# A fused decoder layer (state-space scan, cross attention, quantized FFN) on one core: PSUM slots given job by job in the prologue, side results of the scan taken later

## The chip, the cores and the metric

The kernel runs on one NeuronCore of a Trainium2 chip, as one launch. The metric is the device time of that core in microseconds. The engines are PE (TensorE, matrix multiplies and transposes into PSUM), DVE (VectorE), ACT (ScalarE), POOL (GpSimd) and SP (SyncE, which here issues every DMA). Each engine works through its own instructions in the order in which they are written and waits on semaphores for the others.

## The reference

The input is 8 x 128 x 256 in float32. The state-space block takes the first axis as its time (8 steps) and the 128 rows as its batch; the attention takes the first axis as its batch. A tile t = 0..7 below is one entry of that first axis, 128 rows.

```python
def reference(x, ctx_512, ...):
    x = _layernorm(x + attn_ref(x, ...))        # state-space block
    x = _layernorm(x + xattn_ref(x, ctx, ...))  # cross attention, 16 heads, rope, latent q and k
    x = _layernorm(x + ffn_ref(x, w_up, w_down))# Hadamard, 8-bit activations, ternary weights

def attn_ref(...):
    xz = einsum('ed,lbd->bel', in_proj_w, h);  x, z = split(xz)
    x  = silu(sum_k conv_w[:, k] * shift(x, k))           # 4 taps
    x_dbl = einsum('ed,bdl->bel', x_proj_w, x)            # 128 low-rank rows, 16 B, 16 C
    delta = softplus(dt_proj_w @ x_dbl[:128] + dt_proj_b)
    A = -exp(A_log)                                       # 512 channels x 16 states
    def step(h, t):
        h = exp(delta_t * A) * h + (delta_t * u_t) * B_t  # 16 states
        y = einsum('bdn,bn->bd', h, C_t)
        return h, y
    y = (scan(step) + x * D) * silu(z)
    return out_proj_w @ y

def weight_quant(w):                                      # used for w_up and w_down
    scale = clip(mean(abs(w)), EPS, None)
    return clip(round(w / scale), -1, 1) * scale
```

## The kernel before

The program has three stages, each written out for every engine: the prologue (0 to about 91 us), the scan (to about 280 us), and the attention with the FFN (to the end).

**Prologue.** PE works through a list `jobs` (L236 to L238; the loop that issues them begins at L395). A job writes one pair of PSUM banks, and there are four pairs. X0 to X3 are the input projection of four channel blocks; Z0 to Z3 the gate projection; DTR the low-rank sum over the four convolved blocks (it waits for `silu_s` k+1 before block k); FF the sum that gives the scales of the ternary weights; DT0 to DT3 the step sizes of two tiles each; BC and BCT the B and C rows and their transpose; UD0 to UD3 the skip term u times D; TU0 to TU3 the transposes of u. A job's pair is its place in the list modulo 4 (`pair`, L251), so a job waits until the job four places ahead of it has been taken out of PSUM; `freed` holds which engine takes it and its count. ACT takes Z (`gates`, L733, a Silu into a two-slot buffer that SP stores to DRAM), DTR (L748) and UD (`skips`, L767, also stored by SP). DVE takes the rest: `biased(p)` (L1088) for DT, `step_inputs(p)` (L1112) for TU.

`squares_of(p)` (L753, ACT: Abs, Exp, four Squares) and `softplus(p)` (L1096, DVE: L1103, three times L1105, L1107, L1110) make delta of two tiles, p = 0..3. Square 0 of p waits for L1107 of p-1, since both use one buffer. `ternary(i)` (L1079, DVE, three operations of 1024) rounds w_up (i = 0) and w_down (i = 1). Silu and Exp need different tables of ACT, so there is a table load at each change between `gates` and `squares_of`.

SP stores gates and skips in a written order, then issues `zeros` (2 MB into Nw), `load_m(0)` and `load_m(1)`, waits for all stores to have landed, and only then issues `stage(0)`: the loads of `ud_t` (the stored skip term of the tile), `zs_t` (its gates) and `x_t`.

**Scan.** Seven steps, t = 1..7, of 16 states each. Per state n of step t:

- POOL `arg` (L973): delta times A for two states at a time, into a ring of four;
- ACT `decay(t, n)` (L779): Exp, into one of four PSUM banks; it waits until the state four back has been added;
- DVE `state_decay` (L1160, L1157 in step 1) and `state_add` (L1167): the new state;
- ACT `weigh(t, n)` (L787): state times C into the ring `hc` of four slots; it is issued three states late (`BEHIND`), and waits until PE has used the state four back (`y_s`);
- PE `state_sum` (L497): four transposes that add it onto the tile's sum in PSUM.

PE begins a step with `skip_sum(t)`, which waits for the load of `ud_t` (`st_u`) and for DVE's `gate(t-1)` (L1175, after state 3), since the sum's bank is only free then. After `state_sum` of n = 3 PE does `out_proj(t-1)`, after n = 11 `turn_x1(t-1)`. DVE's norm of the tile before stands after n = 9 and n = 11. I call the start of L1175 the gate of a step; the time from gate to gate is the length of a step.

Four side jobs per step prepare the attention's merged weights: P0 to P3 (step 1), KV0, KV1, N0, N1 (step 2), N2 to N5 (step 3), M0 to M15 (steps 4 to 7). PE issues side job i of a step after the `state_sum` of state `PE_SIDE[i]`, and ACT takes its result (`take_side`, L815; the copies are L825 to L839) after the `decay` and `weigh` of iteration `ACT_SIDE[i]`. Two banks alternate.

SP's order in the scan's iteration t: `stage(t)` (ud_t after `skip_sum(t-1)`, zs_t after `gate(t-1)`, x_t after `out_proj(t-1)`); loads of w_q and w_kcq for later M jobs that wait for side job 0 or 1 of this step; the store of x1; in t = 1 the loads of w_qr and w_kr, which wait for P3; then the loads that wait for side job 2 or 3 (in t = 4, 5 and 6, for M3, M7 and M11).

**Attention and FFN.** PE `project` (L594) waits first for every side result (`pe.wait_ge(side_e, len(side))`). These 32 slots and the FFN are untouched but for one insertion.

```python
PE_SIDE = (0, 4, 8, 10)
ACT_SIDE = (5, 9, 13, 15)
```

## Time and profile before

| | us |
|---|---|
| median of three runs | 568.6 (565.62 to 569.82) |
| the profiled execution's own time | 569.41 |
| its span | 567.2 |
| PE busy (share of the span) | 453.4 (80%) |
| DVE busy | 401.4 (71%) |
| ACT busy | 311.0 (55%) |
| POOL busy | 216.7 (38%) |
| mean granted clock of PE, 1 is 2.4 GHz | 0.874 |

The span runs from the first to the last instruction; 2.2 us lie around it. A wait in brackets behind an instruction is its engine's idle time and what ended it. "PE ps L386" is every matmul that is issued through one helper; its tile names tell the job. A matmul of float32 counts as two records.

### The profile page before, as it was taken

How to read it: one execution, taken by the hardware profiler on the slowest of the kernel's cores; microseconds unless marked ns; L12 is line 12 of the kernel's file. 1: busy time of each engine (PE TensorE's matmuls, PEld its weight loads, DVE VectorE, ACT ScalarE, POOL GpSimd, SP SyncE). 2: the span in 40 equal slices, each digit the busy share in tenths (PEclk: the TensorE clock that was granted, in tenths of full speed). 3: DMA queues.
4: the chain of work that ended last, by engine and by line, in shares of the span. 5: the costliest groups of instructions: out<-in, count | busy, mean ns of one | idle time of the engine just before them, and what ended most of it. 6: DMA issues, size and time to landing. Idle time of an engine off the chain costs nothing.

```text
span 567.2 us, 9787 instructions
## 1 busy us (share of the span) xinstructions
PE 453.4 (80%) x3240; PEld 368.8 (65%) x3248; DVE 401.4 (71%) x722; ACT 311.0 (55%) x717; POOL 216.7 (38%) x157
## 2 busy tenths in 40 slices
PE   4999622858787757566799999999999999998733
PEld 2446422547575645546688889898888888897522
DVE  0949499788678879797754567777777677777443
ACT  2548782769587869696524353444545353444310
POOL 2300037495839486876042323123223223223010
PEclk9999855877575969897999999999999999999765
DMA  8960491040101123031200000000000000000000
GB/s 288 360 223 37 138 337 40 13 121 25 34 9 46 54 68 103 20 102 29 70 20 2 10 1 2 19 0 18 0 18 0 0 18 0 18 0 20 0 9 9
DMA packets 18649, 32.38 MB, mean 57 GB/s; under 512 B 2112, under 2 KB 11712, under 8 KB 17792
## 3 DMA queue, kind: packets, MB, share of 16 engines
q1 hardware_dynamic: 18624, 32.06, 17.0%
q8 instruction: 14, 0.23, 0.2%
q14 instruction: 11, 0.09, 0.1%
HBM read 25.73 MB, written 6.32 MB: 57 GB/s over the span
## 4 chain that ended last, share of the span: by engine, by line
PE 40%; DVE 24%; issue 19%; ACT 10%; POOL 4%; DMA 1%; DVEq 1%; POOLq 0%; ACTq 0%; SPq 0%
PE ps L386 32%; PE ps L497 5%; DVE reg_b L1167 4%; ACT hc L787 4%; DVE reg_b L1105 3%; DVE ps L1160 2%; POOL reg_b L999 2%; PE ps L594 2%; ACT ps L779 2%; ACT reg_b L869 2%; POOL small L978 1%; DVE reg_b L1220 1%; DVE ps L1157 1%; DMA Nw<-x_fm 1%; DVE reg_b L1219 1%
## 5 line engine op out<-in xcount | busy, mean ns | idle before, releaser
L973 POOL TENSOR_TENSOR reg_b<-reg_c,reg_a 128x1024 f32<-128x1024 f32 x56 | 131.1, 2370 | 82.4 <-DVE reg_c L1110 61.1
L999 POOL TENSOR_TENSOR reg_b<-reg_b 128x768 f32<-128x768 f32 x32 | 58.0, 1813 | 140.1 <-DVE reg_b L1220 107.4
L497 PE MATMUL ps<-ident,hc 128*128 128x128 f32 x452 | 86.2, 331 | 29.0 <-ACT hc L787 28.8
L497 PEld LDWEIGHTS ps<-ident,hc 128*128 128x128 f32 x452 | 62.7, 169 | 48.5 <-ACT hc L787 45.1
L386 PE MATMUL ps<-x1T,Mw 128*128 (+1 forms) x768 | 93.5, 278 | 0.0
L386 PEld LDWEIGHTS ps<-x1T,Mw 128*128 128x128 f32 x768 | 88.2, 192 | 3.4 <-issue 0.6
L787 ACT ACTIVATE hc<-reg_b,bc 128x512 f32<-128x512 f32 x112 | 79.8, 713 | 12.8 <-DVE reg_b L1167 12.3
L1160 DVE TENSOR_TENSOR ps<-ps,reg_b 128x512 f32<-128x512 f32 x96 | 66.0, 691 | 26.1 <-ACT ps L779 26.1
L1167 DVE SCALAR_TENSOR_TENSOR reg_b<-reg_c,bc,ps 128x512 f32<-128x512 f32 x112 | 81.9, 736 | 0.0
L869 ACT ACTIVATE reg_b<-ps,small 128x128 f32<-128x128 f32 x128 | 45.3, 366 | 40.0 <-DVE small L1225 39.3
L779 ACT ACTIVATE ps<-reg_b 128x512 f32<-128x512 f32 x112 | 65.7, 588 | 0.7 <-POOL reg_b L973 0.7
L386 PE MATMUL ps<-reg_b,Nw 128*64 128x128 f32 (+1 forms) x512 | 55.7, 283 | 0.3 <-POOL reg_b L999 0.3
L978 POOL TENSOR_TENSOR small<-small 128x1 f32<-128x1 f32 x24 | 13.2, 550 | 110.8 <-DVE small L1185 110.8
L876 ACT ACTIVATE reg_b<-ps 128x512 f32<-128x512 f32 x32 | 19.1, 597 | 63.3 <-PE ps L594 63.3
L386 PEld LDWEIGHTS ps<-reg_b,Nw 128*64 128x64 f32 (+1 forms) x512 | 45.3, 165 | 7.0 <-issue 3.8
L386 PE MATMUL ps<-reg_b 128*64 128x128 f32 (+1 forms) x512 | 43.5, 294 | 2.7 <-ACT reg_b L863 0.5
L497 PE MATMUL ps<-ident,ud_t 128*128 128x128 f32 x32 | 8.9, 434 | 40.8 <-DVE yT L1175 24.9
L386 PEld LDWEIGHTS ps<-reg_b 128*64 128x64 f32 (+1 forms) x512 | 32.3, 166 | 12.5 <-ACT reg_b L863 8.0
L1225 DVE TENSOR_REDUCE small<-ps 128x4 f32<-128x512 f32 x32 | 22.0, 688 | 22.6 <-PE ps L386 22.5
L386 PE MATMUL ps<-Nw 128*128 128x512 f32 x64 | 30.0, 627 | 7.2 <-DMA Nw<-x_fm 7.1
L497 PEld LDWEIGHTS ps<-ident,ud_t 128*128 128x128 f32 x32 | 5.7, 217 | 43.9 <-DVE yT L1175 22.4
L1219 DVE TENSOR_TENSOR reg_b<-ps,reg_a 128x768 f32<-128x768 f32 x32 | 30.4, 951 | 2.9 <-PE ps L386 2.9
(137 smaller groups left out, 714.2 us busy)
## 6 DMA issues: line engine op xcount, KB each, us to landing
reg_a<-a_dram SPq DMA_DIRECT2D x4, 1024.0 KB, 7.9
Mw<-w_o SPq DMA_DIRECT2D x1, 2048.0 KB, 16.2
zs_dram<-x1T SPq DMA_DIRECT2D x4, 512.0 KB, 3.7
ud_dram<-reg_b SPq DMA_DIRECT2D x4, 512.0 KB, 3.0
Nw<-zeros SPq DMA_DIRECT2D x1, 2048.0 KB, 9.6
mring<-w_q SPq DMA_DIRECT2D x8, 256.0 KB, 3.1
ud_t<-ud_dram SPq DMA_DIRECT2D x8, 256.0 KB, 3.5
zs_t<-zs_dram SPq DMA_DIRECT2D x8, 256.0 KB, 3.4
```

What stands on the lines that cost most here:

```text
L386: return pe.matmul(o, l, r, start=start, stop=stop)
L497: return pe.matmul(o, src, ident[:, :], start=start, stop=stop, is_transpose=True, skip_group_check=True)
L779: act.activation(ps[:, n % RING, :], dA[:, n // SA % RING, n % SA, :], ACT.Exp, scale=-1.0).then_inc(da_s, 1)
L787: act.activation(hc[:, (n + 1) % WRING, :], H[:, n, :], ACT.Copy, scale=bc[:, t, s:s + 1]).then_inc(hc_s, 1)
L869: last = act.activation(prob[:, g % 2, h, :], scores_of[:, h % 2, h // 2, :], ACT.Exp, bias=negm[:, g % 2, h:h + 1], accum_out=sums[:, g % ...
L876: act.activation(probT[:, g % 2].rearrange("p h n -> p (h n)"), ps[:, 4, :], ACT.Copy).then_inc(pte, 1)
L973: pool.tensor_tensor(dA[:, g % RING], delta_r[:, bass.ds(t, 1), :].to_broadcast([P, SA, DI]), Abc[:, g * SA:(g + 1) * SA, :], ALU.mult).th ...
L999: pool.tensor_tensor(rq[:, g % 2].rearrange("p a c n -> p (a c n)"), pc[:, g % 2].rearrange("p a c n -> p (a c n)"), psn[:, g % 2].rearran ...
L1160: dve.tensor_tensor(E_n, E_n, H[:, n, :], ALU.mult).then_inc(dah_s, 1)
L1167: dve.scalar_tensor_tensor(H[:, n, :], step_du(t), step_b(t, n), ps[:, n % RING, :], ALU.mult, ALU.add).then_inc(h_s, 1)
L1219: dve.tensor_tensor(pc[:, g % 2], v, ropeq_s[:, 0], ALU.mult)
L1225: dve.tensor_reduce(negm[:, g % 2].rearrange("p (i e) -> p e i", e=2), scores_of, AX.X, ALU.max, negate=True).then_inc(mx, 1)
```

## The change

- `jobs` has a new order, with DTR directly behind X3, Z0 and Z1 behind UD1, Z2 and Z3 behind TU1, and each job's pair of banks is now given in a table, `slot_of`. A job waits for the last holder of its pair.
- ACT's order in the prologue: the gates 0 and 1, then skips 2 and 3, then both remaining `squares_of`, then gates 2 and 3. SP stores in the same order.
- DVE: `ternary(0)` stands ahead of `biased(0)`; `ternary(1)` has left the prologue. Its weights are loaded again after the scan (SP, 512 KB), and it runs between the first and the second eight-slot group of the attention.
- POOL waits for all four deltas before its first `arg`, no longer for the first alone.
- Scan: PE issues side jobs after states 4, 8, 12, 15; ACT takes them in iterations 11 and 15 of the step and 2 and 6 of the next (the last two of all after the scan).

```diff
-PE_SIDE = (0, 4, 8, 10)
-ACT_SIDE = (5, 9, 13, 15)
+PE_SIDE = (4, 8, 12, 15)
+ACT_SIDE = (11, 15, NST + 2, NST + 6)
...
-        jobs = row("X", *range(CI)) + row("Z", 0) + row("DTR", 0) + row("FF", 0) + row("DT", 0, 1) + row("BC", 0)
-        jobs += row("DT", 2) + row("BCT", 0) + row("DT", 3) + row("UD", 0, 1, 2) + row("Z", 1, 2, 3) + row("UD", 3)
-        jobs += row("TU", *range(T // 2))
+        jobs = row("X", *range(CI)) + row("DTR", 0) + row("FF", 0) + row("DT", 0, 1, 2) + row("BC", 0)
+        jobs += row("DT", 3) + row("BCT", 0) + row("UD", 0, 1) + row("Z", 0, 1) + row("UD", 2, 3)
+        jobs += row("TU", 0, 1) + row("Z", 2, 3) + row("TU", 2, 3)
+        slot_of = dict(zip(jobs, (0, 1, 2, 3, 0, 1, 3, 1, 0, 2, 3, 1, 3, 1, 2, 0, 3, 1, 3, 1, 2, 0, 3, 1)))
...
-                if j >= 4:
-                    who, n = freed[jobs[j - 4]]
+                if before[job]:
+                    who, n = freed[before[job]]
...
-            store_gates(0)
             store_skip(0)
             store_skip(1)
+            store_gates(0)
+            store_gates(1)
             store_skip(2)
-            for p in range(1, CI):
-                store_gates(p)
             store_skip(3)
+            store_gates(2)
+            store_gates(3)
             sp.wait_ge(pe_job, pos[("Z", CI - 1)] + 1)
             sp.dma_start(nw_flat, zeros).then_inc(ld["zero"], 16)
...
             sp.dma_start(had_s, had).then_inc(ld_had, 16)
+            sp.dma_start(wdn_again, w_dn).then_inc(ld_wdn, 16)
...
-            gates(0)
             gated(3)
...
             squares_of(0)
             skips(0)
+            skips(1)
             squares_of(1)
-            skips(1)
+            gates(0)
+            gates(1)
             skips(2)
+            skips(3)
             squares_of(2)
-            gates(1)
+            squares_of(3)
             gates(2)
             gates(3)
-            skips(3)
-            squares_of(3)
...
                     if n in ACT_SIDE:
                         take_side(per_step * (t - 1) + ACT_SIDE.index(n))
+                    if carried and NST + n in ACT_SIDE:
+                        take_side(per_step * (t - 2) + ACT_SIDE.index(NST + n))
...
+            for j in range(len(side) - sum(n >= NST for n in ACT_SIDE), len(side)):
+                take_side(j)
             take_x1(T - 1)
...
-            pool.wait_ge(delta_s, 1)
+            pool.wait_ge(delta_s, T // 2)
...
+            ternary(0, wup_raw, wupq[:, :, :])
             biased(0)
             biased(1)
+            biased(2)
             take(("BC", 0))
...
-            ternary(0, wup_raw, wupq[:, :, :])
-            biased(2)
+            biased(3)
             take(("BCT", 0))
...
-            ternary(1, wdn_raw, wdnq[:, :, :])
+            softplus(1)
...
             slots(0, True, False, False, lag=False, scan_end=True)
+            dve.wait_ge(ld_wdn, 16)
+            ternary(1, wdn_again, wdnq[:, :, :])
             slots(1, True, True, False)
```

PE in the prologue, before. `Nw 128x512` is X or Z (four rows a job), `reg_b,Pw 128x512` DTR, `small,x` FF, `zs_t,Pw` DT (two a job), `32x256` BC, `x_t` BCT, `ud_t,reg_b` UD (eight a job), `ident,reg_b` TU (eight a job):

```order
L386 MATMUL ps<-Nw 128x512 x20
L386 MATMUL ps<-reg_b,Pw 128x512 x8
L386 MATMUL ps<-small,x 128x2
L386 MATMUL ps<-zs_t,Pw 128x512 x4
L386 MATMUL ps<-reg_b,Pw 32x256 x16
L386 MATMUL ps<-zs_t,Pw 128x512 x2
L428 MATMUL ps<-ident,x_t 128x128 x2
L386 MATMUL ps<-zs_t,Pw 128x512 x2
L386 MATMUL ps<-ud_t,reg_b 128x128 x24
L386 MATMUL ps<-Nw 128x512 x12
L386 MATMUL ps<-ud_t,reg_b 128x128 x8
L456 MATMUL ps<-ident,reg_b 128x128 x32
```

The same engine and place in the changed kernel:

```order
L396 MATMUL ps<-Nw 128x512 x16
L396 MATMUL ps<-reg_b,Pw 128x512 x8
L396 MATMUL ps<-small,x 128x2
L396 MATMUL ps<-zs_t,Pw 128x512 x6
L396 MATMUL ps<-reg_b,Pw 32x256 x16
L396 MATMUL ps<-zs_t,Pw 128x512 x2
L438 MATMUL ps<-ident,x_t 128x128 x2
L396 MATMUL ps<-ud_t,reg_b 128x128 x16
L396 MATMUL ps<-Nw 128x512 x8
L396 MATMUL ps<-ud_t,reg_b 128x128 x16
L466 MATMUL ps<-ident,reg_b 128x128 x16
L396 MATMUL ps<-Nw 128x512 x8
```

Z0 has left the place ahead of DTR, and the first two TU jobs now stand ahead of Z2 and Z3; the last two TU jobs follow these rows.

ACT in the prologue, before, from the Squares of p = 0 on (L764 Squares, L770 skips, L757 and L759 Abs and Exp, L736 gates):

```order
L764 ACTIVATE reg_b<-reg_b,small 128x1024 x4
L770 ACTIVATE reg_b<-ps 128x1024 x2
L757 ACTIVATE reg_b<-reg_c 128x1024
L759 ACTIVATE reg_b<-reg_b 128x1024
L764 ACTIVATE reg_b<-reg_b,small 128x1024 x4
L736 ACT_TABLE_LOAD
L736 ACTIVATE x1T<-ps 128x1024 x3
L770 ACTIVATE reg_b<-ps 128x1024
L757 ACTIVATE reg_b<-reg_c 128x1024
L759 ACT_TABLE_LOAD
L759 ACTIVATE reg_b<-reg_b 128x1024
L764 ACTIVATE reg_b<-reg_b,small 128x1024 x4
```

ACT in the changed kernel, from the Squares of p = 1 on (L773 Squares, L779 skips, L766 and L768 Abs and Exp, L746 gates):

```order
L773 ACTIVATE reg_b<-reg_b,small 128x1024 x4
L746 ACT_TABLE_LOAD
L746 ACTIVATE x1T<-ps 128x1024 x2
L779 ACTIVATE reg_b<-ps 128x1024 x2
L766 ACTIVATE reg_b<-reg_c 128x1024
L768 ACT_TABLE_LOAD
L768 ACTIVATE reg_b<-reg_b 128x1024
L773 ACTIVATE reg_b<-reg_b,small 128x1024 x4
L766 ACTIVATE reg_b<-reg_c 128x1024
L768 ACTIVATE reg_b<-reg_b 128x1024
L773 ACTIVATE reg_b<-reg_b,small 128x1024 x4
L746 ACT_TABLE_LOAD
```

Both pairs of gates now come with a table load of their own; gates 2 and 3 are behind every Square.

PE in step 1 of the scan, before (`ident,ud_t` skip_sum, `ident,hc` state_sum, four a state, `Mw 64x256` a P job, `w_out_s,yT` out_proj):

```order
L497 MATMUL ps<-ident,ud_t 128x128 x4
L497 MATMUL ps<-ident,hc 128x128 x4
L386 MATMUL ps<-Mw 64x256 x4
L497 MATMUL ps<-ident,hc 128x128 x12
L386 MATMUL ps<-w_out_s,yT 128x256 x4
L497 MATMUL ps<-ident,x_t 128x128 x2
L497 MATMUL ps<-ident,hc 128x128 x4
L386 MATMUL ps<-Mw 64x256 x4
L497 MATMUL ps<-ident,hc 128x128 x16
L386 MATMUL ps<-Mw 64x256 x4
```

The same step in the changed kernel, from out_proj to its end:

```order
L396 MATMUL ps<-w_out_s,yT 128x256 x4
L507 MATMUL ps<-ident,x_t 128x128 x2
L507 MATMUL ps<-ident,hc 128x128 x4
L396 MATMUL ps<-Mw 64x256 x4
L507 MATMUL ps<-ident,hc 128x128 x16
L396 MATMUL ps<-Mw 64x256 x4
L507 MATMUL ps<-ident,hc 128x128 x12
L540 MATMUL ps<-ident,x 128x128 x2
L507 MATMUL ps<-ident,hc 128x128 x4
L396 MATMUL ps<-Mw 64x256 x4
L507 MATMUL ps<-ident,hc 128x128 x12
L396 MATMUL ps<-Mw 64x256 x4
```

No job stands ahead of out_proj any more, and the fourth one is now the last thing in the step, directly ahead of the next skip_sum. SP's own order in the scan is the same in both.

## Rows read from the trace of the kernel before

**Rows 1.** Gate to gate: length; PE, PEld, DVE, ACT, POOL busy; PE clock; DMA share, GB/s

```profile
96.72:123.90 27.18, 19.18 (x112) 12.99 (x112) 22.67 (x39) 20.76 (x37) 19.07 (x10) 0.81 0.28 68
123.90:151.00 27.10, 21.94 (x104) 18.26 (x104) 22.22 (x39) 21.13 (x39) 20.27 (x10) 0.63 0.09 31
151.00:181.40 30.40, 25.01 (x112) 20.17 (x112) 22.24 (x39) 22.59 (x44) 19.22 (x10) 0.61 0.10 26
...
206.90:232.50 25.60, 16.72 (x96) 13.70 (x96) 22.03 (x39) 20.34 (x37) 19.22 (x10) 0.89 0.23 67
...
258.02:279.58 21.56, 16.78 (x98) 13.98 (x99) 16.49 (x29) 15.47 (x28) 6.90 (x4) 0.87 0.21 65
```

**Rows 2.** The page's costliest groups: busy, mean ns, idle before and its releaser

```profile
L1160 DVE TENSOR_TENSOR ps<-ps,reg_b 128x512 f32<-128x512 f32 x96 | 66.0, 691 | 26.1 <-ACT ps L779 26.1
```

**Rows 3.** Timeline, start of step 7: start, us, engine, line, [idle before <-releaser]

```profile
258.75 1.12 PE L497 MATMUL ps<-ident,ud_t 128*128 128x128 f32 x4 [3.48 <-DVE yT L1175]
259.66 1.06 PE L497 MATMUL ps<-ident,hc 128*128 128x128 f32 x4
260.51 1.49 PE L386 MATMUL ps<-mring 128*128 128x192 f32 x4
...
262.04 0.49 ACT L839 ACTIVATE Mw<-ps 128x384 f32<-128x384 f32 x1 [4.44 <-PE ps L386]
```

**Rows 4.** Timeline of the prologue, the same columns

```profile
26.27 7.03 PE L386 MATMUL ps<-reg_b,Pw 128*128 128x512 f32 x16
...
27.39 1.05 ACT L730 ACTIVATE reg_b<-reg_b 128x1024 f32<-128x1024 f32 x1
...
45.16 0.68 DVE L1103 TENSOR_SCALAR reg_b<-reg_b 128x1024 f32<-128x1024 f32 x1
...
49.66 1.23 DVE L1107 TENSOR_TENSOR reg_b<-reg_b 128x1024 f32<-128x1024 f32 x1
...
60.16 4.26 ACT L764 ACTIVATE reg_b<-reg_b,small 128x1024 f32<-128x1024 f32 x4 [1.06 <-DVE reg_b L1107]
...
65.74 1.94 ACT L736 ACTIVATE x1T<-ps 128x1024 f32<-128x1024 f32 x2
66.81 3.67 PE L456 MATMUL ps<-ident,reg_b 128*128 128x128 f32 x16 [5.12 <-ACT x1T L736]
68.82 1.23 DVE L1115 TENSOR_TENSOR reg_c<-ps,reg_c 128x1024 f32<-128x1024 f32 x1 [7.50 <-PE ps L456]
```

**Rows 5.** Timeline, the end of the prologue, the same columns

```profile
77.26 5.11 POOL L973 TENSOR_TENSOR reg_b<-reg_c,reg_a 128x1024 f32<-128x1024 f32 x2 [54.79 <-DVE reg_c L1110]
78.00 2.18 DVE L1103 TENSOR_SCALAR reg_b<-reg_b 128x1024 f32<-128x1024 f32 x1
80.21 5.76 DVE L1105 SCALAR_TENSOR_TENSOR reg_b<-reg_b 128x1024 f32<-128x1024 f32 x3
90.79 1.42 DVE L1157 SCALAR_TENSOR_TENSOR ps<-ps,bc,reg_c 128x512 f32<-128x512 f32 x2
90.81 1.12 PE L497 MATMUL ps<-ident,ud_t 128*128 128x128 f32 x4 [15.92 <-DVE reg_c L1115]
```

**Rows 6.** SP's queue: start and duration of an issue

```profile
72.51 0.89 SPq L321 DMA_DIRECT2D Nw<-zeros  x1
77.16 0.33 SPq L332 DMA_DIRECT2D ud_t<-ud_dram  x1
114.50 0.51 SPq L352 DMA_DIRECT2D Mw<-w_qr  x1
115.69 0.58 SPq L332 DMA_DIRECT2D ud_t<-ud_dram  x1
```

**Rows 7.** ud_t loads issued at 77.16, 115.69, 249.43: KB, us from issue to landing

```profile
ud_t<-ud_dram SPq DMA_DIRECT2D x1, 256.0 KB, 7.9
ud_t<-ud_dram SPq DMA_DIRECT2D x1, 256.0 KB, 6.8
ud_t<-ud_dram SPq DMA_DIRECT2D x1, 256.0 KB, 3.6
```

More of the change, by code:

```diff
@@ L165, in decoder_layer @@
         x2_new = reg_a[:, 1792:1792 + DM]
+        wdn_again = reg_a[:, 2048:3072]
         off = [0]
@@ L215, in decoder_layer @@
         x1Tm = sem("x1Tm"); x1Te = sem("x1Te"); x1_out = sem("x1_out")
-        ld_rope = sem("ld_rope"); ld_had = sem("ld_had")
+        ld_rope = sem("ld_rope"); ld_had = sem("ld_had"); ld_wdn = sem("ld_wdn")
         xa_s = sem("xa_s"); ropem = sem("ropem"); radd = sem("radd"); qmm = sem("qmm")
@@ L249, in decoder_layer @@
             freed[(kind, c)] = (who, tally[who])
+        before = {}
+        held = {}
+        for job in jobs:
+            before[job] = held.get(slot_of[job])
+            held[slot_of[job]] = job
         def pair(job):
-            return ps[:, 2 * (pos[job] % 4):2 * (pos[job] % 4) + 2, :]
+            return ps[:, 2 * slot_of[job]:2 * slot_of[job] + 2, :]
         def flat(job):
@@ L776, in decay @@
                 need(act, h_s, NST * (t - 1) + n + 1 - RING)
-                if t == 1 and n in (0, 2):
-                    act.wait_ge(dve_free, freed[("TU", n // 2)][1])
+                if t == 1 and n == 0:
+                    act.wait_ge(act_free, freed[("Z", CI - 1)][1])
+                if t == 1 and n == 2:
+                    act.wait_ge(dve_free, freed[("TU", T // 2 - 1)][1])
                 act.activation(ps[:, n % RING, :], dA[:, n // SA % RING, n % SA, :], ACT.Exp,
@@ L823, in take_side @@
                     if c == 0:
-                        act.wait_ge(ffq, 2)
+                        act.wait_ge(ffq, 1)
                     last = act.activation(kvT[:, c * (T // 2):(c + 1) * (T // 2), :].rearrange("p t n -> p (t n)"), o,
@@ L984, in scan_step @@
                 for g in range(AG):
-                    if isinstance(t, int) and t == 1 and g == 2:
-                        pool.wait_ge(soft_s, 5 * (T // 2))
-                        pool.wait_ge(delta_s, T // 2)
                     arg(t, g)
@@ L1128, in _ @@
                             ).then_inc(dve_free, 1)
-            biased(3)
             softplus(0)
@@ L1132, in _ @@
             dve.tensor_tensor(cb_n[:, :], bc[:, 0, 0:NST], bc[:, 0, NST:2 * NST], ALU.mult).then_inc(cb_s, 1)
-            ternary(1, wdn_raw, wdnq[:, :, :])
+            softplus(1)
             dve.wait_ge(cb_s, 1)
             dve.tensor_reduce(cb0, cb_n[:, :], AX.X, ALU.add).then_inc(cb_s, 1)
-            softplus(1)
             step_inputs(0)
```

## The prediction

> **What bounds the kernel now.** I read first the stages gate to gate [rows 1]. In the scan's steps DVE is busy for 22.0 to 22.7 us whatever the step lasts (25.6 to 30.4), so this is the floor of a step; POOL with 19 us and ACT with 20 to 23 us are near it but under it. PE's busy time follows its clock: 16.7 us at 0.89, 25.0 us at 0.61. Then the costliest groups [rows 2]: DVE idles 26.1 us of steps 2 to 7 before L1160, all of it for ACT's decay. The timeline of a step's start says why [rows 3]. The gate is at 258.02; PE starts `skip_sum` 0.73 later, sums state 0, then does the M job, whose record begins at 260.51; ACT, which has to take that job in iteration 5, stands still for 4.44 us and starts at 262.04. No decay is issued meanwhile, and DVE runs dry for some 3 us. Steps 4 to 6 are alike (25.5 us each; 206.90 stands for three). In the prologue [rows 4] DVE waits 7.50 us at 68.82 for the transpose of TU0, PE waits 5.12 us for a pair of banks that ACT holds, and ACT is late with the gates (65.74) since they stand behind four Squares. At its end [rows 5] DVE's operations are slow next to POOL.
>
> **Prologue, up to the start of the scan (90.79 before).** Z0 ahead of DTR is gone: 8 records at 0.44 us, 3.5 us. But block 3 of DTR needs the last silu, which ended at 28.44 [rows 4] and hardly moves; DTR's last quarter (1.76 us) ends at 30.2 instead of 33.3. With the new order of DT2, BC and DT3 behind it I let `softplus(0)` start at 42.5 instead of 45.16. A softplus is 4.50 us up to L1107 (45.16 to 49.66), then two operations of 1.23: 7.0 us. Square 0 of the next comes after L1107.
> From there ACT leads. It does an operation of 1024 in 1.07 us (4.26 for four), a copy out of PSUM in 0.97 (1.94 for two), a table load in 1.3 (the gap from 64.42 to 65.74). Skips 0 and 1 wait for two UD jobs behind `biased(3)` (42.2): an estimate of 1.8 us each, from a TU job's half of 3.67, and they end at 47.0. Abs and Exp: 49.1; Squares 1 to 53.4; so DVE's `softplus(1)` runs 50.2 to 57.2. ACT: table 54.7, gates 0 and 1 56.6, skips 2 and 3 58.5, Abs, table, Exp 61.9, Squares 2 to 66.2. TU0 is on time now, so that the 7.50 us go; but `softplus(2)` waits for ACT until 63.0 and ends at 70.0. Squares 3 end at 73.2; `step_inputs(1)` and `softplus(3)` end at 78.2, at its undisturbed 7.0 us: beside POOL its L1103 took 2.18 us where it took 0.68, and its three L1105 5.76 us where 3.75 is the pace of the first (45.16 to 49.66) [rows 4, 5]. Two more `step_inputs` (2.4) and, beside them, POOL's first pair of args (2.5, half of 5.11) and one decay: the scan begins at 81.4, 9.4 us earlier.
> The rule of the Trainium skill that bears on this ("SBUF — State Buffer", the practical consequences on the shared port pair): a DVE instruction in a two-port mode or with two SBUF inputs and a reading GpSimd instruction exclude each other for whole instructions. The trace agrees with 2.18 against 0.68 us. By it the moved `ternary(1)` is exposed to the rope sum on GpSimd; that would add under 2 us once.
>
> **The end of the prologue on SP.** Most of the 9.4 us does not arrive. Gates 2 and 3 now stand behind Squares 3: 73.2, table, two gates, 76.4. SP's store of gates 3, and with it `zeros`, the m loads and `stage(0)`, wait for this. Before, `zeros` went out at 72.51, ud_t at 77.16, and it landed 7.9 us later, 12.5 us after `zeros` [rows 6, 7]. Now `zeros` goes at 76.9, ud_t lands at 89.0 (89.4 less a little, since one store fewer is in the queues). `skip_sum(0)` and the first state_sum take 1.97 us (cold), the gate of tile 0 comes at 91.0 instead of 87.4; before, it was at 96.72. **Gain 5.7 us.** This is insensitive to errors in the DVE chain, as the load is last there.
>
> **Scan.** The wait of ACT for the side job at the start of the step goes. What is late next is `weigh(4)`, which needs `state_sum` 0 of the step: with `skip_sum` at +0.73 it ends at +2.70 [rows 3], the decay of state 8 is ready at +4.1, and DVE reaches it at 0.6 for the gate and three states of 1.26 behind it, +4.4 (an estimate: 22.1 us less some 1.9 for gate and norm, over 16 states). So 0.3 us of slack: a clean step is DVE's 22.1 us. Then out_proj: `weigh(8)` needs `state_sum` 4 behind it. With the clock at 2.4 GHz that just fits; at 1.2 GHz out_proj takes about twice as long and DVE waits 1 to 2 us. The clock was at its lower level for part of each step; I take 0.5 us per step for it, more in steps 1 to 3.
> But the fourth side job now ends a step, and SP has loads waiting for it *ahead of the next ud_t*. The last state_sum ends 2.75 us before the gate (3.48 idle less 0.73 [rows 3]).
> - Into step 2: P3 (1.1 us) ends 1.7 before the gate, w_qr and w_kr are issued in 1.2 us [rows 6], ud_t goes at -0.4 and lands 6.8 us later behind that 1 MB [rows 7]: +6.4, where `skip_sum` wants it at +0.73. 5.7 late, less the 0.3: 5.4 us.
> - Into steps 5, 6, 7 (M3, M7, M11 release the m loads): the M job ends 2.1 (warm) to 1.4 (cold) before the gate, two issues about 1.0, landing 3.6 [rows 7]: +2.5 to +3.2, so 1.5 to 2.2 us of stall. I take 1.8.
>
> Lengths: step 1, DVE 22.7, ud_t(1) late (issued once `skip_sum(0)` has ended, 0.9 us of stall), cold out_proj 1.4: 25.0 (before 27.18, **-2.2**). Step 2: 22.2 + 5.4 + 1.3 = 28.9 (27.10, **+1.8**). Step 3, with slow N jobs: PE's busy 25.0, less the last job (2.0, now in the idle time before the gate), plus 2.7 of that idle time: 25.7 (30.40, **-4.7**). Step 4: 22.7 (25.5, **-2.8**). Steps 5 and 6: 22.1 + 1.8 + 0.4 = 24.3 (**-1.3, -1.3**). Step 7: 21.56 - 3.3 + 1.9 = 20.2 (**-1.4**). Together 11.9 us.
> Added behind the scan: M15 and its copy now lie after the last sum and ahead of `project`: 0.7 + 0.5 + 0.2 of handing over, **+1.4**. `ternary(1)` is three operations of 0.68, 2.1 us on DVE between two slots in which PE is the bound; a slot has room for most: **+0.3** (0 to 4 by the rule above). The load of 512 KB lies beside the end of the scan: nothing. In the prologue `ternary(1)` is already gone in the sum.
>
> **Sum.** 5.7 + 11.9 - 1.7 = 15.9 us from 569.41, 553.5; the profiled execution lies 0.8 above the median, so **553 us** beside 568.6.
>
> **Rivals.**
> 1. *ud_t costs less than I say.* If the loads behind the last side job land in parallel with what is in front of them, or ACT and DVE run further ahead than I count, steps 2, 5, 6, 7 are clean and the start of the scan keeps half its 3.6 us: 5.4 + 5.4 + 1.8 = 12.6 less: 540.4. For it: the queues are hardly used elsewhere. Against it: 6.8 and 7.9 us in rows 7, where 1 MB or more was ahead. A half-way 547 is as likely as the whole.
> 2. *The clock.* Three jobs that stood at the start and middle of a step are later, and the burst ahead of out_proj is transposes alone. If out_proj and the jobs behind it run at 1.2 GHz in every step, as in the step at 151.00 (0.61, 25.0 us of PE), steps 4 to 7 lose 1.5 us each and steps 1 to 3 3 us together: 562. For it: the lower level after each idle time at a gate. The Trainium skill ("TensorE: Matmul & The Clock Gate", on oscillation) says that idle gaps throttle the engine again. In the trace, that gap is 3.48 us before and gets longer wherever ud_t is late.
> 3. *Slower: PE becomes the engine of the scan.* At 1.2 GHz throughout, a step is 17 sums and skip at 0.98, out_proj and x_t 3.9, three jobs of 1.5 to 2.0, turn_x1 0.6, 2.7 of waiting for the gate: 29 us. It decides once more than four of seven steps are cold from end to end; with all seven, 7 x 29 less 183 is 20 more, less 5.7, plus 1.7: 585. Against it: the mean clock is 0.81 or more in five steps of seven [rows 1].
> 4. *No effect (566).* Half of rival 2 together with POOL or the prologue eating the start: only if `softplus` and ACT's chain are slower by 6 us than counted.
>
> **Chances.** Forecast (548 to 558) 0.52; rival 1 0.20; rival 2 0.18; rival 3 0.04; rival 4 0.06. Faster by over 1% (under 562.9, about what a measurement of this kernel can tell from no change): all of the first two, most of the third, 0.87. Within 1%: 0.08. Slower: 0.05. The range holds 8 in 10: 540 to 563, from the whole of rival 1 to the whole of rival 2.
>
> **What would show it.** Right: DVE's first scan operation near 81.4, but the first L1175 near 91, with PE waiting for a DMA before its first L497; in steps 5 to 7 PE's idle time before ud_t's transposes ended by a DMA, two us longer than now; in step 2 above 5 us of it; gate-to-gate lengths near 25, 29, 26, 23, 24, 24, 20; no 4.4 us of ACT before a side copy; L1103 four times at 0.68. Wrong: PE's wait at the gate still ended by DVE's yT (then rival 1); clock at 0.5 over the whole of a step after step 3 (rivals 2, 3); a first gate later than 93 (then the ACT chain is mis-sized).

## The result, and the profile after

| | before | after |
|---|---|---|
| median, us (range, runs) | 568.69 (565.62 to 569.82, 4) | 544.83 (543.67 to 548.26, 4) |
| profiled execution, us (its span) | 569.41 (567.2) | 543.67 (541.5) |
| first gate / last gate, us | 96.72 / 279.58 | 92.83 / 254.18 |
| behind the last gate, to the span's end | 287.6 | 287.3 |
| mean granted clock | 0.874 | 0.914 |

The ratio is 0.9582, with a 95% interval of 0.9544 to 0.962. So 23.9 us went by the medians, where 15.6 us were forecast. Between the two profiled executions it was 25.7 us: 3.9 us ahead of the first gate, 21.5 us between the gates, 0.3 us behind them. A second set of runs of the same kernel (below) gave 0.9559 [0.9503, 0.9615].

Line numbers below are those of the kernel after: the gate is L1187, the state sums and skip_sum are L507, the jobs L396, the decays and their use L790 and L1172 (L1169 in step 1), delta L1116, L1118, L1120 and L1123.

The stages gate to gate, steps 1, 2, 3, 5 and 7, with the columns of [rows 1]:

```profile
92.83:116.48 23.65, 18.09 (x112) 13.79 (x112) 22.67 (x37) 19.66 (x36) 18.33 (x10) 0.84 0.15 42
116.48:144.07 27.59, 16.54 (x104) 14.23 (x104) 21.94 (x38) 20.44 (x39) 18.43 (x10) 0.81 0.28 70
144.07:166.84 22.77, 18.80 (x112) 15.88 (x112) 21.95 (x38) 21.98 (x43) 19.97 (x10) 0.82 0.13 35
...
189.07:212.03 22.96, 16.16 (x96) 14.04 (x96) 21.95 (x39) 20.09 (x38) 19.20 (x10) 0.85 0.25 76
...
235.26:254.18 18.92, 14.61 (x94) 12.91 (x95) 16.40 (x30) 15.42 (x29) 6.88 (x4) 0.91 0.37 119
```

DVE's busy time has hardly moved; the lengths have come down to it. In step 3 30.40 us became 22.77, at 21.95 of DVE: the floor is reached but for 0.8 us. PE's busy time fell by 5 to 6 us in steps 2 and 3 at the same count of instructions, since its clock rose from 0.63 and 0.61 to 0.81 and 0.82. What is left stands in step 2, in which no engine is busy for more than 21.94 of 27.59 us.

The costliest groups, the answer to [rows 2]; below it the group of ud_t's transposes on PE:

```profile
L1172 DVE TENSOR_TENSOR ps<-ps,reg_b 128x512 f32<-128x512 f32 x96 | 65.7, 690 | 8.8 <-ACT ps L790 8.7
...
L507 PE MATMUL ps<-ident,ud_t 128*128 128x128 f32 x32 | 8.7, 426 | 46.4 <-DMA ud_t<-ud_dram 42.0
```

DVE's wait for decays fell from 26.1 to 8.8 us. PE's wait ahead of ud_t's transposes is now ended by a DMA, 42.0 of 46.4 us, where in [rows 3] it was DVE's gate. It is so at six of the eight tiles (17.7 us of it ahead of the first gate, the rest in steps 1, 2, 5, 6 and 7); in steps 3 and 4 DVE's gate still ends it. The timeline, PE at the first gate and at the starts of steps 1, 2 and 5, then SP's issues of ud_t for the first tile and for steps 2 and 5:

```profile
90.85 1.09 PE L507 MATMUL ps<-ident,ud_t 128*128 128x128 f32 x4 [17.74 <-DMA ud_t<-ud_dram]
...
94.67 0.66 PE L507 MATMUL ps<-ident,ud_t 128*128 128x128 f32 x2 [1.88 <-DMA ud_t<-ud_dram]
...
123.11 1.09 PE L507 MATMUL ps<-ident,ud_t 128*128 128x128 f32 x4 [8.76 <-DMA ud_t<-ud_dram]
...
191.07 1.09 PE L507 MATMUL ps<-ident,ud_t 128*128 128x128 f32 x4 [4.56 <-DMA ud_t<-ud_dram]
...
82.10 0.33 SPq L341 DMA_DIRECT2D ud_t<-ud_dram  x1
...
115.59 0.58 SPq L341 DMA_DIRECT2D ud_t<-ud_dram  x1
...
187.39 0.43 SPq L341 DMA_DIRECT2D ud_t<-ud_dram  x1
```

The gates of these steps are at 116.48 and 189.07. In step 2 ud_t goes out 0.9 before the gate and PE starts 6.6 behind it; in step 5 it goes out 1.7 before and PE starts 2.0 behind. DVE's queue takes up part of that: its wait in step 2 is 5.46 us, in step 5 0.84.

DVE in the prologue and at the start of the scan, the answer to [rows 4, 5]:

```profile
59.20 1.22 DVE L1128 TENSOR_TENSOR reg_c<-ps,reg_c 128x1024 f32<-128x1024 f32 x1 [0.98 <-PE ps L466]
63.46 0.69 DVE L1116 TENSOR_SCALAR reg_b<-reg_b 128x1024 f32<-128x1024 f32 x1 [3.03 <-ACT reg_b L773]
...
71.88 0.68 DVE L1116 TENSOR_SCALAR reg_b<-reg_b 128x1024 f32<-128x1024 f32 x1
72.60 3.74 DVE L1118 SCALAR_TENSOR_TENSOR reg_b<-reg_b 128x1024 f32<-128x1024 f32 x3
...
82.17 1.42 DVE L1169 SCALAR_TENSOR_TENSOR ps<-ps,bc,reg_c 128x512 f32<-128x512 f32 x2 [1.04 <-ACT ps L790]
92.83 0.69 DVE L1187 TENSOR_TENSOR yT<-ps,zs_t 128x512 f32<-128x512 f32 x1 [4.40 <-PE ps L507]
```

The wait of 7.50 us became 0.98; 2.18 and 5.76 us beside POOL became 0.68 and 3.74. DVE begins the scan 8.6 us earlier and then waits 4.40 us at the first gate.

### The profile page after: what moved, and what is told of

Read it like the earlier page. It is cut to its first block, busy times and chain, and to the rows that moved or that the text cites. A ratio compares the mean times of both kernels' runs of the same rounds, so it can differ in the third digit from the quotient of the medians.

```text
span 541.5 us, 9797 instructions
## 1 busy us (share of the span) xinstructions
PE 434.6 (80%) x3248; PEld 358.3 (66%) x3248; DVE 397.5 (73%) x722; ACT 312.8 (58%) x719; POOL 216.0 (40%) x157
## 4 chain that ended last, share of the span: by engine, by line
PE 39%; issue 19%; DVE 14%; ACT 14%; DMA 7%; POOL 6%; SPq 1%; DVEq 1%; POOLq 0%; ACTq 0%
PE ps L396 31%; PE ps L507 5%; DMA ud_t<-ud_dram 5%; ACT hc L798 3%; POOL reg_b L1012 2%; ACT ps L790 2%; PE ps L604 2%; DVE ps L1172 2%; POOL reg_b L989 2%; DVE reg_b L1179 2%; POOL small L994 2%; ACT reg_b L773 2%; ACT reg_b L885 1%; DVE reg_b L1232 1%; DMA Nw<-x_fm 1%
## 5 line engine op out<-in xcount | busy, mean ns | idle before, releaser
L396 PE MATMUL ps<-x1T,Mw 128*128 (+1 forms) x768 | 93.6, 278 | 0.6 <-ACT Mw L851 0.6
L396 PEld LDWEIGHTS ps<-x1T,Mw 128*128 128x128 f32 x768 | 88.2, 192 | 4.3 <-ACT Mw L851 0.9
L507 PE MATMUL ps<-ident,hc 128*128 128x128 f32 x452 | 75.3, 315 | 16.0 <-ACT hc L798 15.8
L507 PEld LDWEIGHTS ps<-ident,hc 128*128 128x128 f32 x452 | 61.2, 163 | 27.2 <-ACT hc L798 26.3
L1172 DVE TENSOR_TENSOR ps<-ps,reg_b 128x512 f32<-128x512 f32 x96 | 65.7, 690 | 8.8 <-ACT ps L790 8.7
L790 ACT ACTIVATE ps<-reg_b 128x512 f32<-128x512 f32 x112 | 65.4, 585 | 4.1 <-POOL reg_b L989 4.1
L396 PE MATMUL ps<-reg_b,Nw 128*64 128x128 f32 (+1 forms) x512 | 55.2, 281 | 0.2 <-POOL reg_b L1012 0.2
L396 PEld LDWEIGHTS ps<-reg_b,Nw 128*64 128x64 f32 (+1 forms) x512 | 45.0, 164 | 7.0 <-issue 3.8
L507 PE MATMUL ps<-ident,ud_t 128*128 128x128 f32 x32 | 8.7, 426 | 46.4 <-DMA ud_t<-ud_dram 42.0
L396 PE MATMUL ps<-reg_b 128*64 128x128 f32 (+1 forms) x512 | 42.1, 287 | 2.8 <-ACT reg_b L879 0.5
L396 PEld LDWEIGHTS ps<-reg_b 128*64 128x64 f32 (+1 forms) x512 | 31.2, 161 | 12.3 <-ACT reg_b L879 8.0
L507 PEld LDWEIGHTS ps<-ident,ud_t 128*128 128x128 f32 x32 | 5.7, 213 | 48.6 <-issue 43.8
L396 PE MATMUL ps<-Nw 128*128 128x512 f32 x64 | 30.3, 632 | 7.3 <-DMA Nw<-x_fm 7.3
L1231 DVE TENSOR_TENSOR reg_b<-ps,reg_a 128x768 f32<-128x768 f32 x32 | 30.4, 951 | 4.4 <-PE ps L396 4.4
```

Source lines behind the costliest of these rows:

```text
L396: return pe.matmul(o, l, r, start=start, stop=stop)
L507: return pe.matmul(o, src, ident[:, :], start=start, stop=stop, is_transpose=True, skip_group_check=True)
L790: act.activation(ps[:, n % RING, :], dA[:, n // SA % RING, n % SA, :], ACT.Exp, scale=-1.0).then_inc(da_s, 1)
L1172: dve.tensor_tensor(E_n, E_n, H[:, n, :], ALU.mult).then_inc(dah_s, 1)
L1231: dve.tensor_tensor(pc[:, g % 2], v, ropeq_s[:, 0], ALU.mult)
```

## The experiments

Two parts alone, two edits of SP's queue that take the new wait away, three edits that put back or shift one thing, combinations, and the changed kernel again. A name stands for one kernel; times are medians, ratios against the kernel before in the same set of runs. All gates, read off the timeline of each profile:

| kernel | first gate | steps 1 to 7 | last gate | behind it |
|---|---|---|---|---|
| before | 96.72 | 27.18 27.10 30.38 25.49 25.60 25.55 21.56 | 279.58 | 287.6 |
| after | 92.83 | 23.65 27.59 22.77 22.23 22.96 23.23 18.92 | 254.18 | 287.3 |
| after_again | 92.51 | 23.57 27.51 22.76 22.22 22.88 22.80 17.99 | 252.24 | 288.8 |
| scan_only | 97.57 | 22.69 27.35 22.78 22.22 22.83 23.09 18.16 | 256.69 | 288.6 |
| prologue_only | 91.74 | 28.37 27.10 30.38 26.10 25.61 25.86 21.58 | 276.74 | 287.2 |
| ud_first | 92.90 | 23.12 22.05 22.78 22.22 22.04 22.04 18.01 | 245.16 | 291.7 |
| start | 89.11 | 22.68 27.22 22.77 22.23 22.81 22.96 18.84 | 248.62 | 287.3 |
| both | 88.45 | 22.67 22.05 22.76 22.23 22.03 22.04 18.46 | 240.69 | 290.3 |
| pool_early | 96.75 | 23.17 27.19 22.77 22.21 22.83 22.92 18.13 | 255.97 | 288.5 |
| ternary_back | 92.65 | 23.27 27.07 22.76 22.22 22.82 23.10 18.00 | 251.89 | 288.6 |
| sides_earlier | 93.64 | 23.29 24.71 22.61 22.35 22.03 22.04 17.99 | 248.66 | 287.5 |
| both_sides | 89.19 | 22.67 22.05 23.21 22.34 22.04 22.04 17.99 | 241.53 | 287.5 |
| both_pool_early | 91.57 | 22.74 22.05 23.41 22.22 22.03 22.04 17.99 | 244.05 | 292.0 |

**scan_only: the scan's part alone,** in the kernel before, with the lines of ACT that take a result in the next step.

```diff
-PE_SIDE = (0, 4, 8, 10)
-ACT_SIDE = (5, 9, 13, 15)
+PE_SIDE = (4, 8, 12, 15)
+ACT_SIDE = (11, 15, NST + 2, NST + 6)
```

> Theory A (the parts are independent; the scan's gain is the removed wait of ScalarE at the start of a step): the first gate stays at 96.7 us, the seven steps take about 160.5 us instead of 182.9, the part behind the last gate 1.5 us more; so about 21 us less than the kernel before, 548 us. ScalarE's 4.4 us before each first side copy are gone; PE waits for the ud_t load in steps 2, 5, 6, 7. Theory B (the scan gains only together with the new prologue, since there the steps start with another phase of the clock and the loads): 12 us less or fewer, 556 us or more.

Measured: 546.5 us, ratio 0.9625 [0.955, 0.97]. Steps 2 to 6 are those of the changed kernel within 0.3 us each (step 1 is 1.0 shorter, step 7 0.8), the late ud_t of step 2 included. The second row of it, with the columns of [rows 1]:

```profile
120.26:147.61 27.35, 16.70 (x104) 14.36 (x104) 21.94 (x38) 20.32 (x39) 18.79 (x10) 0.81 0.28 69
147.61:170.39 22.78, 17.22 (x112) 14.72 (x112) 21.96 (x39) 22.01 (x43) 19.97 (x10) 0.90 0.13 35
```

So the rise of the clock in steps 2 and 3 comes with the positions of the side jobs alone.

PE's and ACT's positions moved together here and were not tried apart. What the timeline of the kernel before shows is where DVE waited: 30.4 us in the seven steps, 22.9 of them for the first decay behind ACT's copy of the step's first side result, most of the rest behind its later ones. Those waits are gone.

**prologue_only: the rest alone,** the changed kernel with the old four positions.

> Theory A: the first gate comes at about 92.8 us, held by the ud_t load, the steps are as before (182.9 us): 4 us less than the kernel before, 565 us. Theory B (a large part of the gain comes from the prologue, through what follows it): 8 us less or more, 561 us or below.

Measured: 564.16 us (10 runs), ratio 0.9929 [0.9896, 0.9963]: 4 us, and at the gates 5.0 at the first and 2.8 at the last. Its step 3 is that of before, with the clock of before:

```profile
147.21:177.59 30.38, 24.99 (x112) 20.16 (x112) 22.24 (x39) 22.58 (x44) 19.17 (x10) 0.61 0.09 26
```

The two parts are 21 to 22 us and 4 us, and add up to about the whole (23.9).

**ud_first: ud_t ahead of the loads that wait for a side job.**

```diff
                 store_x1(t - 1)
+                if t + 1 < T:
+                    stage_u(t + 1)
                 if t == 1:
```

(`stage_u` is the load of ud_t taken out of `stage`; those of tiles 0 and 1 stand ahead.)

> The load of ud_t for the next step is issued before the loads that wait for the last side job. Theory A (the late ud_t costs what DVE idles before L1172 in steps 2, 5, 6 and 7: 5.5 + 0.8 + 0.9 + 0.8): 8 us less than the changed kernel, 537 us; PE's wait at these gates is ended by the gate of DVE, 1.6 to 2.8 us long. Theory B (PE at its lower clock is next, so that the time returns as a wait behind out_proj): 3 us less or fewer, 542 us.

Measured: 539.79 us, ratio 0.9507 [0.9442, 0.9572]. Step 2 fell from 27.59 to 22.05, steps 5 to 7 by 0.9 to 1.2 each; the last gate is 9.0 us earlier, and PE's waits in these steps are ended by DVE's gate again:

```profile
116.77 1.12 PE L513 MATMUL ps<-ident,ud_t 128*128 128x128 f32 x4 [2.95 <-DVE yT L1193]
...
183.82 0.66 PE L513 MATMUL ps<-ident,ud_t 128*128 128x128 f32 x4 [3.30 <-DVE yT L1193]
```

The theory holds for the scan. But the median fell by 5.0 only, which is between the two theories: 4.4 us more than in the changed kernel's profile lie behind the last gate, where the kernel is unchanged (see the last section). Against the second profile of the changed kernel (after_again, below) the gain is 7.1 us at the last gate and the loss behind it 2.9; step 7 is then no shorter.

**start: zeros and m loads behind the loads of the first two tiles.**

```diff
-            sp.wait_ge(pe_job, pos[("Z", CI - 1)] + 1)
-            sp.dma_start(nw_flat, zeros).then_inc(ld["zero"], 16)
-            load_m(0)
-            load_m(1)
...
                 stage(t)
+                if t == 1:
+                    sp.wait_ge(pe_job, pos[("Z", CI - 1)] + 1)
+                    sp.dma_start(nw_flat, zeros).then_inc(ld["zero"], 16)
+                    load_m(0)
+                    load_m(1)
```

> The 2 MB of zeros and the first two m loads are issued behind the loads of the first two tiles. Theory A (the first gate is held by that queue alone): the first gate at about 88.5 us instead of 92.8 and ud_t of tile 1 in time: 4.5 to 5 us less than the changed kernel, 540 us. Theory B (the store of the last gates, or VectorE itself, is next at once): 2 us less or fewer.

Measured: 537.4 us, ratio 0.9444 [0.9379, 0.9509]; 7.4 less than the changed kernel by medians, 5.6 by the last gate (3.7 of it at the first gate, 1.0 in step 1). SP, then PE, at the first gate:

```profile
82.17 0.33 SPq L337 DMA_DIRECT2D ud_t<-ud_dram  x1
...
84.97 1.08 PE L508 MATMUL ps<-ident,ud_t 128*128 128x128 f32 x4 [10.21 <-DMA ud_t<-ud_dram]
...
89.90 1.08 PE L508 MATMUL ps<-ident,ud_t 128*128 128x128 f32 x4 [2.99 <-DVE yT L1188]
```

ud_t is issued no earlier than before (82.17 against 82.10), since it waits for the stores of the gates to have landed (SP stands from 78.34 on with nothing else to issue); it lands in 2.7 us instead of 8.6, with the 2 MB of zeros and the m loads no longer ahead of it. DVE then reaches the first gate without waiting for PE.

**both: the two edits together.**

> The changed kernel with both edits on SyncE's queue: ud_t of the next state issued ahead of the loads that wait for the last side job, and the zeros and the first two m loads issued behind the first two states' loads. Theory A: the two waits are apart (one before the first gate, one at the gates of states 1, 5, 6 and 7), so the gains add: first gate near 89.1, steps of 22 to 22.8 us, last gate near 242 (254.2 in the changed kernel), time 531 to 534 us, about 0.936 of the kernel before. Theory B: both edits take the same slack, or VectorE's queue is full already: last gate at 245 or later, time 537 us or more.

Measured: 529.66 us (6 runs), ratio 0.9301 [0.9258, 0.9344], a little under A's 531 to 534; last gate 240.69. The waits were apart, and the gains add (−5.6 and −9.0 by the last gates, −13.5 together). Every step is now within 0.9 us of DVE's busy time but step 7; here steps 2 and 5, and DVE runs through the first gate without a wait:

```profile
111.12:133.17 22.05, 16.99 (x104) 14.41 (x104) 21.86 (x39) 20.70 (x38) 18.90 (x10) 0.85 0.31 74
...
178.16:200.19 22.03, 16.41 (x96) 14.72 (x96) 21.86 (x38) 20.20 (x38) 19.20 (x10) 0.85 0.28 77
```

**pool_early: GpSimd as early as before.**

```diff
-            pool.wait_ge(delta_s, T // 2)
+            pool.wait_ge(delta_s, 1)
```

(The wait for the other deltas stands ahead of the first `arg` that needs them.)

> The changed kernel with GpSimd started as early as in the kernel before (behind the first delta product; the waits for the rest of the decays' inputs stand further on). Theory A: VectorE's products of the prologue slow down again beside GpSimd (from 0.68 us to about 2.2 us for the small one, from 3.7 us to about 5.8 us for the large), VectorE's part of the prologue ends 2 to 4 us later, but the first gate waits for ud_t (issued at 82.10, landed 8.6 us later), so the first gate moves by less than 1.5 us and the time stays within 2 us of 544.8. Theory B: the late start of GpSimd is worth what it takes off VectorE: first gate and time 3 to 4 us later (548 us or more).

Measured: 549.27 us, ratio 0.9675 [0.9607, 0.9743]. My theory A missed, B holds: the first gate is at 96.75, 3.9 us later, although it waits for ud_t as before. DVE, then POOL, then SP:

```profile
64.45 7.81 DVE L1121 SCALAR_TENSOR_TENSOR reg_b<-reg_b 128x1024 f32<-128x1024 f32 x3 [0.41 <-ACT reg_b L773]
...
64.80 6.38 POOL L989 TENSOR_TENSOR reg_b<-reg_c,reg_a 128x1024 f32<-128x1024 f32 x2 [43.52 <-issue]
...
86.04 0.33 SPq L341 DMA_DIRECT2D ud_t<-ud_dram  x1
```

Three operations take 7.81 us where they take 3.74 alone. They stand ahead of the Squares of the last `squares_of`, those ahead of the gates 2 and 3, and these ahead of SP's stores and ud_t: DVE's delay of 4.07 us arrives in full at SP (86.04 against 82.10, in a prologue that was 0.12 us ahead up to there). The Trainium skill ("SBUF — State Buffer", the practical consequences on the shared port pair) has a DVE instruction with two SBUF inputs and a reading GpSimd instruction lock each other out; L1121 is such a one, and the trace agrees with 7.81 against 3.74 us.

**ternary_back: the second ternary in the prologue again.**

```diff
+            ternary(1, wdn_raw, wdnq[:, :, :])
             softplus(1)
...
-            dve.wait_ge(ld_wdn, 16)
-            ternary(1, wdn_again, wdnq[:, :, :])
```

(The second load of the weights goes too, and ACT's first KV result waits for the second ternary.)

> The changed kernel with the second ternary of the down projection's weights back in the prologue, behind the first delta product, and without its second load. Theory A: VectorE waits for ScalarE in the prologue anyway (0.98 us and 3.03 us ahead of its products), and the first gate waits for ud_t, so the first gate moves by less than 0.5 us; behind the last gate 0.2 us come off; time within 1 us of 544.8. Theory B: the ternary stands on the path of the prologue: first gate and time about 2 us later.

Measured: 543.12 us, ratio 0.9548 [0.9502, 0.9593]; first gate 92.65. The first gate moves by 0.2 us only, as in A, but the 2.1 us hide elsewhere than A says. The changed kernel has these two waits ahead of the one of 0.98 us:

```profile
50.77 0.69 DVE L1116 TENSOR_SCALAR reg_b<-reg_b 128x1024 f32<-128x1024 f32 x1 [0.88 <-ACT reg_b L773]
51.88 3.74 DVE L1118 SCALAR_TENSOR_TENSOR reg_b<-reg_b 128x1024 f32<-128x1024 f32 x3 [0.41 <-ACT reg_b L773]
```

With the ternary in front both are gone, and the 0.98 us are 0.23:

```profile
58.49 1.22 DVE L1127 TENSOR_TENSOR reg_c<-ps,reg_c 128x1024 f32<-128x1024 f32 x1 [0.23 <-PE ps L465]
62.74 0.69 DVE L1115 TENSOR_SCALAR reg_b<-reg_b 128x1024 f32<-128x1024 f32 x1 [3.03 <-ACT reg_b L772]
```

That makes 2.0 us; the wait of 3.03 us is untouched. No gain from moving the ternary shows here.

**sides_earlier: side jobs at 4, 7, 10, 13; results at 11, 14, NST + 1, NST + 4.**

> The changed kernel with its side jobs somewhat earlier: TensorE's at 4, 7, 10, 13 instead of 4, 8, 12, 15, ScalarE's results at 11, 14, and 1 and 4 of the next state instead of 11, 15, 2 and 6. Theory A: the loads that wait for the last side result, and ud_t behind them, are issued about 2.5 us earlier, so the waits of 4.4 us at the gates of states 5, 6 and 7 go nearly (steps of 22.0 to 22.3 us), the step with the 8.8 us wait is 2 to 3 us shorter, and the step ahead of the last gate does not get longer: last gate 4 to 6 us earlier (near 249), time about 540 us. Theory B: a side result taken earlier makes ScalarE wait for TensorE again while VectorE waits behind it, as in the kernel before: steps of 23.5 us or more with VectorE's waits ended by ScalarE, time 545 us or more.

Measured: 539.12 us, ratio 0.9485 [0.9441, 0.953]. Theory A: the last side job ends sooner, so ud_t goes out sooner (113.22 instead of 115.59 for step 2), DVE's wait in step 2 falls from 5.46 to 2.13 us, steps 5 and 6 are 22.03 and 22.04, and the last gate 5.5 us earlier. The positions of the change are somewhat too late for SP's order of loads; it is one cause with ud_first, reached from the other side. (Its first gate is 0.8 us later than in the changed kernel, with the same prologue.)

**both_sides: both with these positions.**

> The kernel with both edits of SyncE's queue (ud_t first; zeros and m loads behind the first tiles' loads), and with the side jobs at 4, 7, 10, 13 and their results at 11, 14, and 1 and 4 of the next state. Theory A: steps 1 to 7 are on VectorE's floor of 22.0 to 22.8 us already, so earlier side jobs bring nothing there; they only take the last job and its copy out of the way ahead of the projection (1.4 us): last gate at 240.5 to 241.5 as with both edits, projection's first transposes about 1 us earlier behind it, time within 2 us of 529.7. Theory B: the earlier ScalarE results cost VectorE waits (steps of 23 us), or there is more to be had than the gates show: more than 2 us away.

Measured: 532.12 us, ratio 0.9349 [0.9299, 0.9398]. That is 2.5 us above `both` and so outside A's 2 us, but the two intervals overlap, and no gain shows. The last gate is at 241.53, and the projection starts at 241.59, 0.06 us behind the gate, where in `both` it starts 1.19 us behind its gate:

```profile
240.18 1.31 PE L514 MATMUL ps<-ident,hc 128*128 128x128 f32 x8
241.59 2.94 PE L403 MATMUL ps<-x1T,Mw 128*128 128x128 f32 x24
```

**both_pool_early: both, with GpSimd early.**

> Both edits of SyncE's queue, and GpSimd started as early as in the kernel before. In the kernel with both edits the first gate (88.45) waits for no load but follows VectorE's first state sums without a gap, from 82.27 on. Theory A: the slower VectorE products (7.81 us instead of 3.74 us for three, as in the run of the changed kernel with the early GpSimd) push VectorE's first scan operation to 85.1, first gate near 91.3, 2.8 us later and not 3.9 us, since the wait of 1.0 us for the first decay goes with the earlier GpSimd; time 531 to 534 us. Theory B: without the waiting ud_t the early start costs nothing or pays: first gate 88.5 or earlier.

Measured: 537.96 us, ratio 0.944 [0.9386, 0.9495]; first gate 91.57, last gate 3.4 us later than in `both`, as theory A has it. The median is 8.3 us above that of `both` and outside A's range. Behind the last gate this profile has 292.0 us, that of `both` 290.3; the remaining 3 us no profile shows, since the profiled execution of `both` (533.14) was one of its two long ones, 3.5 us above its median.

**after_again: the changed kernel unaltered.**

> The changed kernel again, unaltered, as the yardstick for the small differences. Theory A: gates within 0.5 us of the first profile, step 1 by up to 0.5 us and step 2 by up to 0.5 us shorter as in all the other runs that keep them; the part behind the last gate 286 to 290 us with the clock in the last 50 us differing; median 543.5 to 546. Theory B: the first profile was not typical, gates more than 1.5 us away.

Measured: 543.82 us, ratio 0.9559 [0.9503, 0.9615]. The first gate is 0.3 us earlier and the last 1.9, beyond A's 0.5 and even B's 1.5: 0.9 of it is step 7, which was 18.92 in the first profile and 17.99 here, with no wait of DVE for a decay. So a difference of up to 1 us in a single step is not by itself an effect. The 0.9 to 1.2 us of steps 5 to 7 in `ud_first` are 0.8, 0.8 and 0.0 against this profile, and what speaks for steps 5 and 6 is DVE's wait there (0.84 and 0.91, here 0.76 and 0.67), which goes. By the last gates `start`, `ud_first` and `both` bring 3.6, 7.1 and 11.6 us against this profile, where against the first they bring 5.6, 9.0 and 13.5; the gains add either way, within about 1 us. The first gate varies as well where nothing ahead of it was altered: from 91.74 (`prologue_only`) to 93.64 (`sides_earlier`).

## Why the prediction was right or wrong

The direction and the main mechanism were right (the wait for the side job goes, a late ud_t comes in its place), and the time lay in the outer range. It did not lie in the forecast's own band of 548 to 558, to which the prediction gave 0.52: the gain was 15.9 by the sum and 25.7 in the profiled executions, and what was too small in the sum is the gain of the steps.

- *Prologue up to the scan (forecast 81.4).* DVE's first operation is at 82.17; softplus(0) at 42.81 (42.5), Squares 1 from 49.59, gates 0 and 1 at 55.16, gates 2 and 3 from 75.24. The chain of ACT was as worked out.
- *"Most of the 9.4 us does not arrive", first gate 91.0.* Right in kind, 1.8 short: 92.83. zeros 77.61 (76.9), ud_t out at 82.10 (81.5) and 8.6 us in landing (7.5). `start` proves the cause: first gate 89.11.
- *"This is insensitive to errors in the DVE chain, as the load is last there."* Wrong, and I still took it over into the expectation of `pool_early`. The load's issue hangs on the DVE chain, through the Squares and the gates. Four first gates tell it: 92.83 with GpSimd late and 96.75 early, 88.45 and 91.57 with the queue mended. With GpSimd early the first gate is where it was before the change (96.72): the new order of the slots alone brings the first gate nothing, with the late GpSimd on top 3.9 us, and with GpSimd early but zeros no longer in front of ud_t 5.2 us (96.72 to 91.57). The late GpSimd in the old order was not run, so what it is worth by itself is open.
- *The wait for the side job goes.* Right, [rows 2]: 26.1 us to 8.8, and `scan_only` has it alone.
- *Late ud_t into step 2: PE at +6.4, DVE 5.4.* Measured +6.6 and 5.46, gone in `ud_first`. The step came out worse than before (27.59 against 27.10), as forecast, with all the rest of it better.
- *Late ud_t into steps 5 to 7, "I take 1.8".* Mis-sized: 0.84 to 0.91 of wait, and 0.9 to 1.2 by `ud_first` (less against the second profile). The M job ended 2.6 us ahead of the gate, not 2.1 to 1.4, so ud_t went out 1.7 ahead and not 1.1 to 0.4. PE's idle time in step 7 grew from 3.48 to 4.39 us and not by the two us named as a sign. That is 2 to 3 us of the error.
- *The clock: "1.4" for a cold out_proj in step 1, "1.3" in step 2, "0.4" to "0.5" in the others, step 3 bound by PE at "25.7".* This is the term of the sum that missed most. Without the waits for ud_t the steps are 22.7, 22.05, 22.8, 22.2, 22.0, 22.0 in `both`: no step pays for the clock more than 0.9 us over DVE's busy time. In step 3 I carried the 0.61 of [rows 1] over; it was 0.82 after. These terms make 6 to 7 us, and with the one above nearly the whole error between the gates: 171.1 forecast, 161.4 measured.
- *Behind the scan, +1.4 and +0.3.* The projection starts 1.19 behind the gate (0.2 ahead of it before), so the 1.4 is there, and `both_sides` takes it away; but 287.3 us follow the last gate where 289.3 were due. The end of the kernel varies by more than that between profiles. Of the 0.3 for `ternary(1)` no run shows a part: its three operations took 0.74, 0.69 and 0.69 us from 279.70 on, as in the prologue before (0.75, 0.69, 0.69), so nothing held them up.
- The sum of the errors: +1.8 (first gate) −9.7 (steps) −2.0 (end) = −9.9, and 553.5 − 9.9 = 543.6.
- *Rivals.* The first (ud_t costs less, 540 to 547, at 0.20) gave the time, but by its mechanism only for the 2 to 3 us of steps 5 to 7: step 2 paid in full, and PE's waits are ended by the DMA, for 42.0 us in all. The clock (562) and PE as the engine of the scan (585) went the other way. No effect (566) is out.

Open: why the clock rises with the new positions. The stretches of 5 us of step 3, before from 151.00 and after from 144.07, with the columns of [rows 1]:

```profile
151.00:156.00 5.00, 4.27 (x18) 3.71 (x19) 1.93 (x4) 0.36 (x2) 2.63 (x2) 0.50 0.22 56
156.00:161.00 5.00, 4.81 (x18) 3.96 (x17) 3.97 (x7) 4.96 (x10) 2.37 (x1) 0.50 0.00 0
161.00:166.00 5.00, 3.93 (x29) 3.28 (x28) 2.29 (x4) 2.54 (x7) 0.00 (x0) 0.99 0.08 26
```

```profile
144.07:149.07 5.00, 4.26 (x22) 4.24 (x23) 5.00 (x10) 4.94 (x10) 5.00 (x3) 0.66 0.21 56
149.07:154.07 5.00, 5.00 (x38) 4.41 (x36) 4.81 (x11) 4.69 (x10) 2.20 (x3) 1.00 0.08 26
```

Both begin behind a similar idle time of PE, and in the kernel before ACT waits for side jobs (4.64 us at 155.74, 2.42 at 163.56) and DVE behind it:

```profile
151.73 1.12 PE L497 MATMUL ps<-ident,ud_t 128*128 128x128 f32 x4 [2.86 <-DVE yT L1175]
...
157.03 0.70 DVE L1160 TENSOR_TENSOR ps<-ps,reg_b 128x512 f32<-128x512 f32 x1 [4.10 <-ACT ps L779]
...
164.85 0.70 DVE L1160 TENSOR_TENSOR ps<-ps,reg_b 128x512 f32<-128x512 f32 x1 [2.71 <-ACT ps L779]
```

```profile
144.81 1.06 PE L507 MATMUL ps<-ident,ud_t 128*128 128x128 f32 x4 [2.75 <-DVE yT L1187]
```

Before, PE stayed at 1.2 GHz for 10 us, and DVE waited 8.0 us in the step, in part for side results that the slow PE owed; after, it is back at 2.4 GHz within 5 us, and DVE is busy throughout (5.00 and 4.81). That the job at the start of the step keeps the clock down was not tried apart from the wait that it causes.

## What to carry to other kernels

When work is taken away from the start of a stage and put at its end, look at what the DMA queue holds back for it: the next stage's first small load stood behind bulk loads that waited for the moved job, and cost 5.5 us in one step; a queue's order is part of such a change. Put a load that the next gate needs ahead of bulk loads that it can spare (2.7 us of landing instead of 8.6), and follow every chain to the *issue* of that load before calling another chain harmless. And do not carry the granted clock of a stage over into a forecast in which the stage is arranged anew: bound the stage by the busy time of the engine that does not depend on the clock.
